# Softmax attention with sixteen heads of eight: TensorE's transpositions and the next batch's projection move ahead of a step's mask and scores

## The reference, cut to what matters

```
qkv = x @ w_attn + b_attn                  # B = 16, T = 256, C = 128
q, k, v = heads(q), heads(k), heads(v)     # 16 heads of 8 channels
q, k = _rope(q), _rope(k)
att = einsum('bhqd,bhkd->bhqk', q, k) / sqrt(8)
att = softmax(where(causal, att, -inf))
y = einsum('bhqk,bhkd->bhqd', att, v)
```

## Time and profile before

| what | value |
|---|---|
| device time, median of 3 runs | 2450.08 us (2448.97 to 2451.7) |
| the profiled execution: span from its first to its last instruction | 2427.7 us |
| mean granted TensorE clock over the span | 0.975 |
| the stage of the change, first mask to the last PV | 215.1 to 547.7 us |
| TensorE busy over the whole span | 2292.7 us, 94% |

### The profile page before, as it was taken

How to read it: one execution, slowest core, us unless ns; L and a number is a source line. 1 busy time by engine, 2 the same in 40 slices (tenths; PEclk the granted TensorE clock), 3 DMA queues, 4 the chain that set the end, 5 groups by cost and what they waited for, 6 DMA issues and landing times. The chain is left out here.

```text
span 2427.7 us, 65264 instructions
## 1 busy us (share of the span) xinstructions
PE 2292.7 (94%) x21510; PEld 1689.7 (70%) x21510; DVE 1861.0 (77%) x4164; ACT 1802.1 (74%) x5994; POOL 1477.1 (61%) x1402
## 2 busy tenths in 40 slices
PE   5898999996898999999999999888999999999999
PEld 3894666663895888845888854774888864888863
DVE  4784888874786999955999964775999964999974
ACT  3455888883447999955999964337999973999982
POOL 5672777774674777733777740432787851878760
PEclk8897999998999999999999999999999999999999
DMA  6111000001112000000000000000000000000000
GB/s 243 45 45 38 2 0 0 0 1 41 45 45 98 7 6 9 4 5 3 8 8 6 6 1 1 1 1 7 8 6 9 6 1 5 11 6 6 9 1 35
DMA packets 34263, 47.49 MB, mean 20 GB/s; under 512 B 6384, under 2 KB 27760, under 8 KB 33744
## 3 DMA queue, kind: packets, MB, share of 16 engines
q1 hardware_dynamic: 29584, 36.45, 4.8%
q0 software_dynamic: 4544, 9.35, 1.2%
HBM read 24.44 MB, written 12.96 MB: 15 GB/s over the span
## 5 line engine op out<-in xcount | busy, mean ns | idle before, releaser
L265 POOL TENSOR_TENSOR space<-space,tabs 128x512 f32<-128x512 f32 x256 | 326.0, 1273 | 286.4 <-DVE space L369 270.0
L289 ACT ACTIVATE space<-psum,space 128x128 f32<-128x128 f32 x1024 | 357.6, 359 | 4.9 <-DVE space L373 4.9
L262 POOL TENSOR_TENSOR space<-space 128x512 f32<-128x512 f32 x256 | 266.2, 1040 | 149.2 <-DVE space L357 149.2
L269 POOL TENSOR_TENSOR space<-space 128x512 f32<-128x512 f32 x256 | 324.8, 1269 | 26.8 <-POOL space L265 7.6
L173 PE MATMUL psum<-space,big 128*128 128x256 f32 x1024 | 264.4, 381 | 10.4 <-DVE space L369 7.2
L1006 POOL TENSOR_TENSOR space<-space 128x256 f32<-128x256 f32 (+1 forms) x256 | 221.1, 884 | 85.5 <-DVE space L1107 83.4
L353 DVE CAST psum<-cb 128x512 f32<-128x512 bf16 x256 | 177.8, 694 | 87.8 <-ACT space L289 87.8
L1051 ACT ACTIVATE space<-psum,space 128x128 f32<-128x128 f32 (+1 forms) x512 | 209.7, 441 | 1.7 <-DVE space L1100 1.7
L196 PE MATMUL psum<-space,cf 128*128 128x384 f32 x512 | 208.6, 489 | 0.0
L289 ACT ACTIVATION_READ_ACCUMULATOR space<-psum,space 128x1 f32 x1024 | 205.3, 200 | 0.0
L173 PEld LDWEIGHTS psum<-space,big 128*128 128x128 f32 x1024 | 175.1, 191 | 29.9 <-issue 16.7
(11 more groups left out here) (193 smaller groups left out, 5636.1 us busy)
## 6 DMA issues: line engine op xcount, KB each, us to landing
big<-early SPq DMA_DIRECT2D x1, 6688.0 KB
space<-sorted_x SPq DMA_DIRECT2D x78, 64.5 KB, 1.9
z<-token_y SPq DMA_DIRECT2D x16, 256.0 KB, 5.6
space<-z SPq DMA_DIRECT2D x64, 64.0 KB, 1.9
space<-z SPq DMA_DIRECT2D x64, 63.8 KB, 2.0
big<-late SPq DMA_DIRECT2D x1, 3114.0 KB, 13.7
x<-x_t SPq DMA_DIRECT2D x4, 512.0 KB, 6.6
x_final<-x SPq DMA_DIRECT2D x8, 256.0 KB, 2.0
```

What stands on the lines that cost most here:

```text
L262: pool.tensor_tensor(x, x, rl[:, (j - 3) % 2, :, :].rearrange("p h t -> p (h t)").unsqueeze(2).to_broadcast([P, 4, P]), ALU.mult).then_inc ...
L265: pool.tensor_tensor(tS[:, :], t2[:, :], tab[:, 1, :], ALU.mult).then_inc(ts_ready, 1)
L269: pool.tensor_tensor(t3[:, j % 2, :], t1[:, j % 2, :], tS[:, :], ALU.add).then_inc(summed, 1)
L289: ins = act.activation(pr[:, (j - 3) % 2, h, t * P:(t + 1) * P], s_ps[h][:, t * P:(t + 1) * P], ACT.Exp, bias=nm[:, (j - 3) % 2, h, t:t + ...
```

## The change

In TensorE's step two blocks move, with their waits, from behind the scores to ahead of the mask: the transpositions of unit s-3, and the projection or the values of the next batch. The order of a step was m, S, projection or values, T, PV; it becomes T, projection or values, m, S, PV. No instruction is added or removed, and no other engine's order changes.

```diff
         def body(i):
             for s, b, k, e in steps(i):
+                u = s - 3
+                if runs(u, U):
+                    kk, ee = place(k, e, 3)
+                    pe.wait_ge(normed, u + 1)
+                    if is_first(u):
+                        prev.free(pe, 6)
+                        prev.free(pe, 7)
+                    if at_least(u, 1):
+                        pe.wait_ge(pt_low, u)
+                        pe.wait_ge(pt_high, u)
+                    for h in range(2):
+                        for c in range(3):
+                            ins = nc.tensor.transpose(pt_ps[h][:, c * P:(c + 1) * P], pr[:, ee % SLOTS, h, c * P:(c + 1) * P], g.ident32)
+                    ins.then_inc(pt_ready, 1)
+
+                if runs(b + 1, B):
+                    if e == 0:
+                        project(b + 1)
+                    if e == 4:
+                        values(b + 1)
+
                 if runs(s, U):
                     jj, bank = e // 2, s_ps[e % 2]
...
                     ins.then_inc(s_ready, 1)
-
-                if runs(b + 1, B):
-                    if e == 0:
-                        project(b + 1)
-                    if e == 4:
-                        values(b + 1)
-
-                u = s - 3
-                if runs(u, U):
...
-                    ins.then_inc(pt_ready, 1)
 
                 u = s - 5
                 if e % 2 and runs(u, U):
```

## The result

The changed kernel takes 2774.23 us (2770.64 to 2774.76, 4 runs) where the kernel before takes 2449.52 us beside it: a ratio of 1.132, with a 95% interval of 1.130 to 1.134. The forecast was 2611.5 us, range 2592 to 2662. So the direction was right, and half of the growth was: the stage grew by 324 us and not by 161.

What follows compares the result with a forecast made beforehand. TensorE's stream was taken to bound the stage; the change closes a 3.68 us loop of waits per step. 123 x 3.68 + 14 x 1.40 = 472.2 us against 310.8, adding 161.4 to 2450.1: 2611.5 us, range 2592 to 2662.

Steps and rivals of the forecast that it cites:

- Bound of the stage: Changed stage, steady part: TensorE's own stream sets the pace, busy 280.00 of 280 us at full clock, 20.03 us a batch.
- The ring: Once per step: scores, VectorE's reductions, reciprocal, copy, then transpositions, mask, next scores; 3.68 us per step at full clock.
- The projection and the values in full view: Between transpositions and mask, inside the closed loop of waits, their 0.91 + 0.49 = 1.40 us a batch is not hidden.
- The clock: Rival: TensorE's clock falls or stays low over most of the stage; 5.27 us a step, 2826 us; 6 in 100.
- a swinging clock: Skill's case: short idles between matmul groups swing TensorE's clock between levels; time between 2611 and 2826 us; no own chance.
- slow steps: Stage's start: return to full clock takes 8 to 16 steps, worth 13 to 25 us; 16 add 25 at the high end.
- GpSimd's chain alone: Rival: only scores, reductions, reciprocal, GpSimd's normalization, transpositions bind; 4.9 us per two steps, 2465 us; 5 in 100.
- faster: Rival: transpositions never wait and the new order saves about 6 us on TensorE, 2444 us; 3 in 100.
- late for nothing: ScalarE's copy and GpSimd's normalization finish before the transpositions ask, so neither adds time; exponentials have one and a half steps.
- The saving from fewer changes of shape: TensorE's array: five shape changes per two steps instead of six, about 0.1 us less per two steps, -6 us.
- The waits: Sign: transpositions wait for VectorE's copy nearly every step, some 1.7 us in even, 0.9 in odd, about 160 in all.
- the signs that were to prove it wrong: Transposition waits naming GpSimd, clock at 0.50 in mid stage, or another mask or scores wait making steps exceed 3.9 us.

## Why the prediction was right and wrong

**Bound of the stage: right.** TensorE's stream set the pace, and with the projection and the values moved alone, which leaves it full, the time stays.

**The ring: right, in place and in size.** The new wait is the transpositions' wait for VectorE's copy of unit s-4, held back behind the reductions of S(s-1). Taking the copy out from behind them removes 287 of 324 us. At the full clock the ring is 3.62 us (forecast 3.68), the growth 159.7 us (forecast 161.4); at the low clock 5.22 (forecast 5.27).

**The projection and the values in full view: right at the full clock only.** In the changed kernel the clock is up for a moment behind them (0.92 for the scores at 303.44), and with them back in the gap it is up less (0.53 against 0.60), so moving them there gained nothing.

**The clock: this step failed.** The prediction priced the low clock at 2826 us and gave it 6 in 100, arguing that "the new gaps are under 2 us and have a group of full work on both sides". That argument is the step that failed. The runs show the opposite: with a gap of 1.7 to 1.8 us in every second step and one of 0.26 us in the others the mean clock is 0.60, and that costs 324 - 160 = 164 us, half of the growth. The time lies between 2611 and 2826, at the place that I had given only to a swinging clock. The rows that should have warned were my own: before the change the stage ran its first 23 us at 0.50 though TensorE was busy for 22.21 of them. Those steps have masks, scores and some transpositions but hardly a product, so it is not the mix of a steady step; still, work of this kind had left the clock low for a long time almost without gaps. I used that row for a price and not for a chance. The Trainium skill (TensorE: Matmul & The Clock Gate, A second HAM failure mode: psum-queue depth-cycling) describes such a case in another kernel, short idles between groups of matmuls that make the clock swing. The trace agrees, with 1.00 in the window at 304 us and 0.50 at 307. I cited it and did not give it the weight.

**The range: too narrow for that reason.** Its upper end allowed 16 slow steps. With a chance for a swinging clock in line with those rows it had to reach to 2826.

**GpSimd's chain alone and faster: refuted as outcomes.** Neither decides the changed kernel. The first shows up once VectorE's copy is out of the way, but beside a ring of ScalarE's that I had dismissed as "late for nothing": true in steps of 3.7 us, not in the shorter ones without VectorE's ring. The saving from fewer changes of shape was never seen.

**Signs that were looked for.** A transposition 0.65 behind the copy's start: seen, 0.58 to 0.66. Even and odd steps alike: seen at the low clock (5.22), but at 5.22 and not 3.7, and a step behind a projection or values is shorter (303.44 to 307.38 is 3.94). The waits: 124 us in 126 of them, 22 under the copy's name and the rest under "issue"; 1.7 in even steps as said, 0.26 and not 0.9 in odd ones, since the product takes longer at the low clock. A batch of 30.8 us: not seen, 40.0 to 41.7. Busy times unchanged: GpSimd's, 245 against 246 us in the stage; VectorE's went from 272 to 258 and ScalarE's from 284 to 301. Of the signs that were to prove it wrong, the clock in mid stage was seen: it reads 0.50 for most of it.

## What to carry to other kernels

When an instruction moves ahead on one engine, look at where its consumers' consumers stand on the other engines: a single buffer whose copy stands behind a wait on the group that was passed closes a ring once per step, and the ring's length is the sum of start-to-start rows, to be compared with TensorE's stream.

Then ask what the new gaps do to TensorE's clock, and give the low level a real chance when the stage already showed it with hardly a gap; here it doubled the damage. To tell the two apart on the chip, fill the gaps with matmuls that nobody needs, and check in the timeline that the ring's other pieces stay as they were: what comes back is the clock's share (here 164 us), what stays is the wait's (here 160).

## What the runs showed of the hardware that I had not expected

Adding work made the kernel faster: 3 matmuls without a use per two steps, 0.50 us by their row, took the changed kernel from a growth of 324 to 177 us, and 10 per two steps to 160.6.

At the low clock TensorE seems busier than it is: its busy share in the stage is 80%, not the "near 70%" of the prediction (its own 20.0 us of work in 30.8 make 65%), since the same matmuls take nearly twice as long. The mean clock has to be read beside the busy share.
